# Both states of a head made by one product, with e^s stationary and k and v side by side

## The chip, the cores and the metric

The kernel runs on one core of a Trainium2 chip. The metric is the device time of one execution in microseconds (us).

## The reference

Input x is (4, 512, 512): 4 sequences of 512 tokens. There are 16 heads, with 128 columns of k and v each and 64 slots. All is float32.

```python
q = rope(x @ Wq.T); k = rope(x @ Wk.T); v = x @ Wv.T; g = x @ Wg.T     # per head (t, 128)
s = clip(x @ Ws1.T @ Ws2.T + bs2, -32, 32)                             # per head (t, 64)
es = exp(s); enz = exp(-cumlogsumexp(s, over t))
A  = tril(q @ k.T) * 128**-0.5
ok = enz * (A @ es)
qv = softmax(ok, over the 64 slots)
W2 = tril((qv * enz) @ es.T)
o  = W2 @ v
o  = o * rsqrt(mean(o * o) + 1e-5) * g_norm_weight * silu(g)
x  = layernorm(x + o @ Wo.T)
x  = layernorm(x + x @ (weight * scale_weight[:, None]).T + bias)
```

## The kernel before

Time is cut into chunks of 128 tokens (P = 128): 4 chunks to a sequence, 16 in all. The heads are cut into 4 groups of 4 heads (HG = 4). One step works on one chunk for one group: 64 steps, numbered i = 1 to 64. Within a sequence c = 0 to 3 is the number of the chunk. Causal sums over earlier chunks are not formed from scratch: after each chunk with c < 3 two states of each head are brought up to date, s1 = sum of k^T e^s (128 x 64) and s2 = sum of (e^s)^T v (64 x 128). A step with c > 0 adds the product of q with s1 to ok, and the product of qv * enz with s2 to o.

Each engine has its program in straight order, and semaphores join them; an engine does nothing out of its order. TensorE's order in `step`: `project_q` of the step after the next (24 matmuls of 256 columns, L958 to L961), ok of the own chunk (L1092), ok from s1 (L1096, c > 0), transposes of o_gated of the step before (L973), in the steps up to i = 14 `low_rank` (L1008), then the projection of k of the next step (L941, 12 matmuls of 512 columns), transposes of ok (L1119), slots, projection of v, transposes of prob, the output projection of the step before, W2 (L1159), o from s2 (L1163), sums of e^s (L986), projection of g, transposes of k_rot, o of the own chunk (L1183), the states (L1188 and L1193, c < 3), and the scores of the next step (L999).

PSUM is eight banks. `bank_c` holds the two accumulators of the states; ACT copies it to `states` in SBUF (L500, 128x512). `bank_e` holds the sums of e^s and their transposes.

The rest of a step that matters here: after L1183 ACT squares o (L662), DVE makes o_gated (L905), sums the squares (L907) and makes var (L910), POOL raises it to the power -1/2 (L461) and multiplies o_gated by it (L463); then o_gated can be transposed (L973) in the next step. DVE masks the scores (`mask_a`, L762) after var, before L1092 can run. In a step with c = 0 DVE then makes the low half of the output weights (L916, 128x2048).

Projections are made in the rounded type float32r, with every factor split into a high and a low half and three products; the matmuls around the states are float32. A matmul with 64 stationary columns writes to 64 of the 128 partitions, and the heads h even and h odd write to different halves.

The states before the change:

```python
for h in range(HG):
    pe.matmul(s1_acc[:, M * h:M * h + M], k_rot[now][:, P * h:P * h + P], es[now][:, M * h:M * h + M], ...)
for h in range(HG):
    mm = pe.matmul(s2_acc[rows, at], es[now][:, M * h:M * h + M], v[now][:, DV * h:DV * h + DV], ...)
```

In `pe.matmul(out, a, b)` a is the stationary operand and b the moving one.

Of the kernel before, what the change touches and what calls it, by code (L numbers as in the profile page):

```python
# [21 lines left out]
P = 128  # L22
# [3 lines left out]
HG = 4  # L26
# [28 lines left out]
def gated_slot_attention_block(nc, hs_cols, hs_rows, w_groups, ws1, small_in, ffn_w, ffn_scale, ffn_bias, out):  # L55
    with ExitStack() as ctx:
# [6 lines left out]
        def sem(name):  # L63
# [25 lines left out]
        masked, o_sq, kT = [sb(n, F)[:, :] for n in ("masked", "o_sq", "kT")]  # L89
        v, gate = [[sb(f"{n}{s}", F)[:, :] for s in range(2)] for n in ("v", "gate")]  # L90
        prob, okT, s_clip = [sb(n, H)[:, :] for n in ("prob", "okT", "s_clip")]
# [6 lines left out]
        rope_a, rope_b = sb("rope_a", F), sb("rope_b", F)  # L98
        k_rot = [sb(f"k_rot{s}", F) for s in range(2)]
        es_hi = [sb(f"es_hi{s}", H, F32R) for s in range(2)]  # L100
# [7 lines left out]

        pT, states = sb("pT", H), sb("states", 2 * H)
        s1, s2 = states[:, 0:H], states[:, H:2 * H]  # L110
        o_gated = sb("o_gated", F)
# [7 lines left out]
            bank(n) for n in ("bank_qv", "bank_kg", "bank_t", "bank_a", "bank_c", "bank_e")]  # L119
        s1_acc, s2_acc = bank_c[:, 0:H], bank_c[:, H:2 * H]  # L120

# [34 lines left out]
        def quarters(t):  # L156
# [3 lines left out]
        x1_bias, y_row, z = [[t[:, :] for t in four] for four in (  # L160
            (qT[0][:, 0:D], k_rot[0], k_rot[1], qT[0][:, D:2 * D]), (kT, v[0], v[1], o_sq), (gate[0], gate[1], masked, rope_a))]
        banks_T, banks_ffn = (bank_c, bank_e, bank_a, bank_s), (bank_qv, bank_kg, bank_t, bank_o)
# [3 lines left out]
        for name in ("first", "second"):  # L166
# [19 lines left out]
            sem(n) for n in ("a_mm", "okT_mm", "w2_mm", "o_mm", "states_mm", "sumT_mm")]  # L186
        kT_mm, pT_mm, ok_mm, oT_mm = [sem(n) for n in ("kT_mm", "pT_mm", "ok_mm", "oT_mm")]
        q_turned, q_summed, k_turned, k_summed = [sem(n) for n in ("q_turned", "q_summed", "k_turned", "k_summed")]
# [105 lines left out]
        def staged(t, s, lag):  # L294

            return t - lag, (s - lag) % LAST, not isinstance(t, int) or 0 <= t - lag < CHUNKS

        block = ctx.enter_context(nc.Block())
# [114 lines left out]
        def _(pool):  # L413
# [13 lines left out]
            def k_sum(slot, n):  # L427
                pool.wait_ge(k_turned, n)
                pool.tensor_tensor(k_rot[slot][:, :], rope_a[:, :], rope_b[:, :], ALU.add).then_inc(k_summed, 1)  # L429

# [67 lines left out]
        def _(act):  # L498
# [76 lines left out]
            hs_split(4)  # L575
            from_bank(v[0][:, :], bank_qv[:, :], v_mm, 1, v_made)
            act.wait_ge(g_mm, 1)
# [34 lines left out]
            def step(u, g, b, c, last, left):  # L612
# [3 lines left out]
                if c % 2 and i + 4 <= STEPS:  # L616
                    hs_split(i + 3)
                if not left:
                    tick(1, 1)
# [18 lines left out]
                if left:  # L638
                    exp_s((c + 1) % 2, n)
                    from_bank(v[(c + 1) % 2][:, :], bank_qv[:, :], v_mm, n, v_made)  # L640
                if last and c == 2:
# [295 lines left out]
        def _(pe):  # L937
# [32 lines left out]

            def transposes(src, n=HG):
                for h in range(n):
                    mm = pe.transpose(bank_t[:, P * h:P * h + P], src[:, P * h:P * h + P], ident)  # L973
                return mm
# [5 lines left out]
            def turn_and_sum(slot, n):  # L980

                pe.wait_ge(es_hi_made, n)
                pe.wait_ge(es_lo_made, n)
                for r in range(2):
                    for x, half in enumerate((es_hi, es_lo)):
                        mm = pe.matmul(bank_e[:, 2 * P * r:2 * P * r + 2 * P], half[slot][:, P * r:P * r + P],  # L986
                                       ident_keep[:, :], start=x == 0, stop=x == 1)
                mm.then_inc(sumT_mm, 1)

            def qT_of(j, h):  # L990
# [51 lines left out]
            pe.wait_ge(k_summed, 1)  # L1042
            transposes(k_rot[0]).then_inc(kT_mm, 1)
            pe.wait_ge(q_turned, 2)
# [23 lines left out]
            def step(u, g, b, c, last, left):  # L1068
# [14 lines left out]
                if not left:  # L1083
                    pe.wait_ge(states_made, carried(u, c - 1))
                    turn_x1(0, 0)
                pe.wait_ge(a_masked, i)
                if c:
                    pe.wait_ge(states_made, carried(u, c - 1))

                for h in range(HG):  # L1090
                    head = slice(P * h, P * h + P)
                    mm = pe.matmul(okT_of(h), es[now][:, M * h:M * h + M], masked[:, head], start=h < 2,  # L1092
                                   stop=c == 0, skip_group_check=True)
                if c:
                    for h in range(HG):
                        mm = pe.matmul(okT_of(h), s1[:, M * h:M * h + M], qT_of(i, h), start=False, stop=True,  # L1096
                                       skip_group_check=True)
                mm.then_inc(okT_mm, 1)

                if i > 1:  # L1100
                    pe.wait_ge(o_norm_made, i - 1)
                    transposes(o_gated).then_inc(oT_mm, 1)
                if i + 2 <= CHUNKS:
                    low_rank(now)
# [55 lines left out]
                if c:  # L1160
                    for h in range(HG):
                        rows, at = slice(64 * (h % 2), 64 * (h % 2) + 64), slice(P * (h // 2), P * (h // 2) + P)
                        mm = pe.matmul(o_of(h), pT[rows, at], s2[rows, at], start=False, stop=False,  # L1163
                                       skip_group_check=True)
                mm.then_inc(w2_mm, 1)
                if left:
                    pe.wait_ge(cumsT_made, 2 * i)
                    turn_and_sum(nxt, n)

                    pe.wait_ge(k_turned, n)  # L1170
                    if last and c == CB - 1:
                        w_ready(g * 4 + 4, g * 3 + 3)
                    project(WG, bank_kg, n).then_inc(g_mm, 1)
                    pe.wait_ge(k_summed, n)
                    transposes(k_rot[nxt]).then_inc(kT_mm, 1)
                if not left:
# [4 lines left out]
                for h in range(HG):  # L1181
                    head = slice(P * h, P * h + P)
                    mm = pe.matmul(o_of(h), masked[:, head], v[now][:, head], start=False, stop=True,  # L1183
                                   skip_group_check=True)
                mm.then_inc(o_mm, 1)
                if c < CB - 1:
                    for h in range(HG):
                        pe.matmul(s1_acc[:, M * h:M * h + M], k_rot[now][:, P * h:P * h + P],  # L1188
                                  es[now][:, M * h:M * h + M], start=c == 0 and h == 0, stop=True,
                                  skip_group_check=True)  # L1190
                    for h in range(HG):
                        rows, at = slice(64 * (h % 2), 64 * (h % 2) + 64), slice(DV * (h // 2), DV * (h // 2) + DV)
                        mm = pe.matmul(s2_acc[rows, at], es[now][:, M * h:M * h + M], v[now][:, DV * h:DV * h + DV],  # L1193
                                       start=False, stop=True, skip_group_check=True)
                    mm.then_inc(states_mm, 1)
# [103 lines left out]
```

## Time and profile before

| What | Value |
|---|---|
| median of 3 runs | 1460.3 us (1459.96 to 1460.4) |
| the profiled execution | 1457.91 us |
| its span, first to last instruction | 1456.1 us |
| TensorE matmuls busy | 1426.3 us (98%), 9664 records |
| DVE, POOL, ACT busy | 951.5, 521.1, 491.3 us |
| mean granted TensorE clock | 0.996 of full speed |

A float32 matmul leaves two records in the trace, one of the rounded type or a transpose one. A record of TensorE begins when its matmul starts; its end is modelled, and records overlap. So the cost of a group is read as the distance from its first start to the first start of the next group.

### The profile page before, as it was taken

The page shows a single profiled execution, that of the slowest core. Times are in us where ns is not written, and L with a number is a line of the kernel's source. Part 1 is how long each engine was busy: PE and PEld are TensorE (multiplying, and loading weights), DVE is VectorE, ACT ScalarE, POOL GpSimd, SP SyncE. Part 2 cuts the span into 40 slices and gives each one's busy share as a digit, 9 for nine tenths or more (in the row PEclk, how much of TensorE's full clock was granted, in tenths as well). Part 3 has the DMA queues.
Part 4 walks back from the last instruction along what each step waited for, and adds up shares of the span by engine and source line. Part 5 has one row for each costly group of instructions (what it writes and reads, how often), then busy time and mean ns, then how long its engine had stood idle before and what let it go on. Part 6 is the DMA issues. An engine that isn't in the chain of part 4 may idle for free.

```text
span 1456.1 us, 23764 instructions
## 1 busy us (share of the span) xinstructions
PE 1426.3 (98%) x9664; PEld 1204.2 (83%) x9664; DVE 951.5 (65%) x1635; ACT 491.3 (34%) x965; POOL 521.1 (36%) x440
## 2 busy tenths in 40 slices
PE   5999999999999999999999999999999999999988
PEld 4888888888888888888888888888888888888876
DVE  5756666566765666567765656657675666657677
ACT  4323223233322323223432322223432222323356
POOL 3322333334433333234533323334432333333255
PEclk9999999999999999999999999999999999999999
DMA  5210111113211201112211110222222021201223
GB/s 203 81 36 33 66 44 59 37 64 120 75 69 44 72 23 55 62 57 97 102 66 30 54 64 26 70 73 67 87 80 66 24 72 44 69 26 66 66 99 118
DMA packets 39562, 97.06 MB, mean 67 GB/s; under 512 B 4384, under 2 KB 4512, under 8 KB 35616
## 3 DMA queue, kind: packets, MB, share of 16 engines
q1 hardware_dynamic: 36864, 90.85, 18.7%
q10 hardware_dynamic: 2592, 4.72, 0.9%
q8 instruction: 76, 1.25, 0.4%
q14 instruction: 30, 0.25, 0.1%
HBM read 74.58 MB, written 20.97 MB: 66 GB/s over the span
## 4 chain that ended last, share of the span: by engine, by line
PE 85%; POOL 7%; DVE 3%; issue 2%; ACT 2%; DMA 0%; POOLq 0%; SPq 0%; ACTq 0%; DVEq 0%
PE bank_kg L941 25%; PE bank_qv L941 13%; PE bank_a L941 12%; PE bank_t L973 6%; POOL o_gated L463 5%; PE bank_wo L1183 4%; PE bank_e L986 3%; PE bank_wo L1159 3%; POOL rms L461 2%; PE bank_a L999 2%; PE bank_qv L958 2%; PE bank_qv L960 2%; PE bank_qv L961 2%; PE bank_c L1188 2%; DVE sum_sq L907 2%
## 5 line engine op out<-in xcount | busy, mean ns | idle before, releaser
L461 POOL TENSOR_TENSOR rms<-var,minus_half 128x4 f32<-128x4 f32 x64 | 65.1, 1017 | 537.3 <-DVE var L910 537.3
L941 PE MATMUL bank_kg<-w_hi,hs_hi 128*128 128x512 f32 x512 | 207.9, 406 | 2.0 <-DVE w_lo L677 1.9
L941 PE MATMUL bank_kg<-w_hi,hs_lo 128*128 128x512 f32 x512 | 202.7, 396 | 0.0
L941 PE MATMUL bank_kg<-w_lo,hs_hi 128*128 128x512 f32 x512 | 201.9, 394 | 0.0
L941 PE MATMUL bank_a<-wo_hi,oT 128*128 128x512 f32 x512 | 174.6, 402 | 0.0
L958 PE MATMUL bank_qv<-hs_hi,w_hi 128*128 128x256 f32 x504 | 146.5, 291 | 9.0 <-DVE w_lo L677 9.0
L758 DVE RECIPROCAL enzT<-cumsT 128x256 f32<-128x256 f32 x64 | 112.2, 1752 | 63.8 <-ACT cumsT L551 51.7
L429 POOL TENSOR_TENSOR k_rot<-rope_a,rope_b 128x512 f32<-128x512 f32 x64 | 82.7, 1292 | 183.4 <-DVE rope_b L706 183.4
L960 PE MATMUL bank_qv<-hs_lo,w_hi 128*128 128x256 f32 x504 | 141.1, 280 | 0.0
L961 PE MATMUL bank_qv<-hs_hi,w_lo 128*128 128x256 f32 x504 | 141.0, 280 | 0.0
L424 POOL TENSOR_TENSOR qT<-rope_a,rope_b 128x512 f32<-128x512 f32 x64 | 82.7, 1292 | 160.7 <-DVE rope_b L718 160.7
L500 ACT ACTIVATE oT<-bank_t 128x512 fp32r<-128x512 f32 x63 | 37.6, 598 | 279.9 <-PE bank_t L973 279.9
L941 PEld LDWEIGHTS bank_kg<-w_hi,hs_lo 128*128 128x128 f32 x512 | 96.1, 188 | 23.1
L941 PEld LDWEIGHTS bank_kg<-w_hi,hs_hi 128*128 128x128 f32 x512 | 96.2, 188 | 22.4 <-issue 3.9
L941 PEld LDWEIGHTS bank_a<-wo_hi,oT 128*128 128x128 f32 x512 | 96.2, 188 | 18.6
L941 PEld LDWEIGHTS bank_kg<-w_lo,hs_hi 128*128 128x128 f32 x512 | 96.3, 188 | 17.6
L941 PE MATMUL bank_qv<-w_hi,hs_hi 128*128 128x512 f32 x256 | 102.7, 401 | 2.8 <-DVE w_lo L677 2.6
L895 DVE TENSOR_TENSOR part<-bank_a,part 128x512 f32<-128x512 f32 x63 | 43.4, 689 | 91.7 <-PE bank_a L941 91.7
L958 PEld LDWEIGHTS bank_qv<-hs_hi,w_hi 128*128 128x128 f32 x504 | 95.2, 189 | 9.0 <-issue 9.0
L941 PE MATMUL bank_qv<-w_lo,hs_hi 128*128 128x512 f32 x256 | 102.2, 399 | 0.0
L941 PE MATMUL bank_qv<-w_hi,hs_lo 128*128 128x512 f32 x256 | 102.1, 399 | 0.0
L418 POOL TENSOR_TENSOR hs_lo<-hs_raw,hs_hi 128x512 fp32r<-128x512 f32 x64 | 97.4, 1523 | 12.3 <-ACT hs_hi L500 12.3
(172 smaller groups left out, 3225.3 us busy)
## 6 DMA issues: line engine op xcount, KB each, us to landing
w_raw<-w_groups SPq DMA_DIRECT2D x28, 1024.0 KB, 5.0
hs_raw<-hs_cols SPq DMA_DIRECT2D x64, 256.0 KB, 2.8
x_scratch<-part SPq DMA_DIRECT2D x64, 256.0 KB, 2.0
part<-x_scratch SPq DMA_DIRECT2D x48, 256.0 KB, 2.8
part<-hs_rows SPq DMA_DIRECT2D x16, 256.0 KB, 3.0
w_raw<-x_scratch SPq DMA_DIRECT2D x16, 256.0 KB, 3.1
w_raw<-w_groups SPq DMA_DIRECT2D x14, 256.0 KB, 6.1
out<-gate ACTq DMA_DIRECT2D x8, 256.0 KB, 2.1
```

The source lines that it names most:

```text
L418: pool.tensor_tensor(in_pair(hs_lo, j), tiles_of(hs_raw[(j - 1) % 2][:, :]), in_pair(hs_hi, j).bitcast(F32), ALU.subtract).then_inc(hs_lo_ ...
L424: pool.tensor_tensor(qT[pair % 2][:, F * half:F * half + F], rope_a[:, :], rope_b[:, :], ALU.add).then_inc(q_summed, 1)
L429: pool.tensor_tensor(k_rot[slot][:, :], rope_a[:, :], rope_b[:, :], ALU.add).then_inc(k_summed, 1)
L461: pool.tensor_tensor(rms[:, :], var[:, :], minus_half[:, :], ALU.pow).then_inc(rms_made, 1)
L463: pool.tensor_tensor(per_head(o_gated[:, :]), per_head(o_gated[:, :]), over_columns(rms[:, :], DV), ALU.mult).then_inc(o_norm_made, 1)
L758: dve.reciprocal(enzT[:, :], cumsT[slot][:, :])
L941: mm = pe.matmul(dst, x, y, start=start and n == 0, stop=stop and n == 2, **kw)
L958: pe.matmul(out_cols, w_hi[WQ][:, w_cols], hi, start=k == 0 and x == 0, stop=False, skip_group_check=True)
L960: pe.matmul(out_cols, w_hi[WQ][:, w_cols], lo, start=False, stop=False, skip_group_check=True)
L961: mm = pe.matmul(out_cols, w_lo[WQ][:, w_cols], hi, start=False, stop=k == KT - 1, skip_group_check=True)
L973: mm = pe.transpose(bank_t[:, P * h:P * h + P], src[:, P * h:P * h + P], ident)
L1183: mm = pe.matmul(o_of(h), masked[:, head], v[now][:, head], start=False, stop=True, skip_group_check=True)
```

## The change

The product with k stationary goes. One product per head has e^s stationary (128 x 64) and k and v side by side moving (128 x 256), and gives both states with the 64 slots on the partitions: (e^s)^T k and (e^s)^T v. For that k (after rotation) and v lie in one buffer `kv`, head by head. s1 is needed with the 128 columns of k on the partitions, so in the next step TensorE turns the k half back with two transposes of 128 x 128 (two heads each) into `bank_e`, and ACT copies the result (128x256) to `s1`. The product of s1 with q (L1096 before) moves behind the transposes of o_gated and waits for that copy.

```diff
-        k_rot = [sb(f"k_rot{s}", F) for s in range(2)]
+        kv = [sb(f"kv{s}", 2 * F)[:, :] for s in range(2)]
-        pT, states = sb("pT", H), sb("states", 2 * H)
-        s1, s2 = states[:, 0:H], states[:, H:2 * H]
+        pT, states, s1 = sb("pT", H), sb("states", 2 * H), sb("s1", H)
-        s1_acc, s2_acc = bank_c[:, 0:H], bank_c[:, H:2 * H]
+        s1_acc = bank_e[:, 0:H]
+        def kv_of(slot, which):
+            return kv[slot].rearrange("p (h e x) -> p h e x", e=2, x=P)[:, :, which, :]
...
-                pool.tensor_tensor(k_rot[slot][:, :], rope_a[:, :], rope_b[:, :], ALU.add).then_inc(k_summed, 1)
+                pool.tensor_tensor(kv_of(slot, 0), per_head(rope_a[:, :]), per_head(rope_b[:, :]), ALU.add).then_inc(k_summed, 1)
...
+                if c:
+                    from_bank(s1[:, :], s1_acc, s1_mm, carried(u, c - 1), s1_made)
                 if not left:
                     tick(1, 1)
...
-                    from_bank(v[(c + 1) % 2][:, :], bank_qv[:, :], v_mm, n, v_made)
+                    from_bank(kv_of((c + 1) % 2, 1), per_head(bank_qv[:, :]), v_mm, n, v_made)
...
-                pe.wait_ge(a_masked, i)
                 if c:
                     pe.wait_ge(states_made, carried(u, c - 1))
+                    pe.wait_ge(cumsT_made, 2 * i)
+                    for r in range(2):
+                        mm = pe.transpose(s1_acc[:, P * r:P * r + P], states[:, 2 * P * r:2 * P * r + P], ident)
+                    mm.then_inc(s1_mm, 1)
+                pe.wait_ge(a_masked, i)
 
                 for h in range(HG):
                     head = slice(P * h, P * h + P)
                     mm = pe.matmul(okT_of(h), es[now][:, M * h:M * h + M], masked[:, head], start=h < 2,
                                    stop=c == 0, skip_group_check=True)
+                if not c:
+                    mm.then_inc(okT_mm, 1)
+
+                if i > 1:
+                    pe.wait_ge(o_norm_made, i - 1)
+                    transposes(o_gated).then_inc(oT_mm, 1)
                 if c:
+                    pe.wait_ge(s1_made, carried(u, c - 1))
                     for h in range(HG):
                         mm = pe.matmul(okT_of(h), s1[:, M * h:M * h + M], qT_of(i, h), start=False, stop=True,
                                        skip_group_check=True)
-                mm.then_inc(okT_mm, 1)
-
-                if i > 1:
-                    pe.wait_ge(o_norm_made, i - 1)
-                    transposes(o_gated).then_inc(oT_mm, 1)
+                    mm.then_inc(okT_mm, 1)
...
-                        mm = pe.matmul(o_of(h), pT[rows, at], s2[rows, at], start=False, stop=False,
+                        mm = pe.matmul(o_of(h), pT[rows, at], s2_of(h), start=False, stop=False,
...
                 if c < CB - 1:
                     for h in range(HG):
-                        pe.matmul(s1_acc[:, M * h:M * h + M], k_rot[now][:, P * h:P * h + P],
-                                  es[now][:, M * h:M * h + M], start=c == 0 and h == 0, stop=True,
-                                  skip_group_check=True)
-                    for h in range(HG):
-                        rows, at = slice(64 * (h % 2), 64 * (h % 2) + 64), slice(DV * (h // 2), DV * (h // 2) + DV)
-                        mm = pe.matmul(s2_acc[rows, at], es[now][:, M * h:M * h + M], v[now][:, DV * h:DV * h + DV],
-                                       start=False, stop=True, skip_group_check=True)
+                        mm = pe.matmul(bank_c[64 * (h % 2):64 * (h % 2) + 64, 2 * P * (h // 2):2 * P * (h // 2) + 2 * P],
+                                       es[now][:, M * h:M * h + M], kv[now][:, 2 * P * h:2 * P * h + 2 * P],
+                                       start=c == 0 and h < 2, stop=True, skip_group_check=True)
                     mm.then_inc(states_mm, 1)
```

`s2_of(h)` is the v half of a head in the new layout of `states`. The buffers of the last phase that shared `k_rot` and `v` share `kv`.

## Rows read from the trace of the kernel before

**Rows 1.** The page, busy us (share of the span) and instructions.

```profile
PE 1426.3 (98%) x9664; PEld 1204.2 (83%) x9664; DVE 951.5 (65%) x1635; ACT 491.3 (34%) x965; POOL 521.1 (36%) x440
```

**Rows 2.** Timeline, POOL and DVE, c = 3: start, duration (us), engine, line.

```profile
705.61 1.04 POOL L463 TENSOR_TENSOR o_gated<-o_gated,rms 128x512 f32<-128x512 f32 x1
...
706.13 1.60 DVE L677 TENSOR_TENSOR w_lo<-w_raw,w_hi 128x1024 fp32r<-128x1024 f32 x1 [0.66 <-ACT w_hi L500]
```

**Rows 3.** Timeline, TensorE, start of the same step with c = 3.

```profile
707.17 0.28 PE L960 MATMUL bank_qv<-hs_lo,w_hi 128*128 128x256 f32 x1
707.29 0.28 PE L961 MATMUL bank_qv<-hs_hi,w_lo 128*128 128x256 f32 x1
707.50 0.66 PE L1092 MATMUL bank_wo<-masked,es 128*64 128x128 f32 x8
707.99 0.61 PE L1096 MATMUL bank_wo<-qT,states 128*64 128x128 f32 x8
708.52 0.66 PE L973 MATMUL bank_t<-small_ops,o_gated 128*128 128x128 f32 x4
708.94 0.48 PE L941 MATMUL bank_kg<-w_hi,hs_hi 128*128 128x512 f32 x1
```

**Rows 4.** Timeline, from c = 0 to c = 1: DVE, POOL, then TensorE.

```profile
745.73 0.16 DVE L910 SCALAR_TENSOR_TENSOR var<-sum_sq,eps_sum 128x4 f32<-128x4 f32 x1
746.30 0.69 DVE L762 TENSOR_TENSOR masked<-bank_a,small_ops 128x512 f32<-128x512 f32 x1 [0.41 <-PE bank_a L999]
746.91 2.34 DVE L916 SCALAR_TENSOR_TENSOR wo_lo<-w_raw,small_ops,wo_hi 128x2048 fp32r<-128x2048 f32 x1
...
746.04 1.02 POOL L461 TENSOR_TENSOR rms<-var,minus_half 128x4 f32<-128x4 f32 x1 [9.37 <-DVE var L910]
747.13 3.02 POOL L463 TENSOR_TENSOR o_gated<-o_gated,rms 128x512 f32<-128x512 f32 x1
...
749.51 0.61 PE L1096 MATMUL bank_wo<-qT,states 128*64 128x128 f32 x8
750.21 0.66 PE L973 MATMUL bank_t<-small_ops,o_gated 128*128 128x128 f32 x4
```

**Rows 5.** Timeline, TensorE, end of a step with c = 2.

```profile
702.06 1.00 PE L1188 MATMUL bank_c<-es,k_rot 128*128 128x64 f32 x8
702.99 0.66 PE L1193 MATMUL bank_c<-v,es 128*64 128x128 f32 x8
...
703.58 0.38 PE L999 MATMUL bank_a<-qT,kT 128*128 128x128 f32 x1
```

**Rows 6.** Timeline, four narrow windows, TensorE: the first start is the next record's.

```profile
318.68 0.33 PE L1193 MATMUL bank_c<-v,es 128*64 128x128 f32 x2
...
318.84 0.50 PE L1193 MATMUL bank_c<-v,es 128*64 128x128 f32 x6
...
318.95 0.39 PE L1193 MATMUL bank_c<-v,es 128*64 128x128 f32 x4
319.27 0.38 PE L999 MATMUL bank_a<-qT,kT 128*128 128x128 f32 x1
```

**Rows 7.** Line L1188: duration ns, minimum/median/maximum.

```profile
L1188 PE MATMUL bank_c<-es,k_rot x384: 222/275/276, 53.7 to 1381.1; 128*128 128x64 f32 x192
```

**Rows 8.** Timeline, TensorE: transposes of k_rot.

```profile
722.77 0.60 PE L973 MATMUL bank_t<-small_ops,k_rot 128*128 128x128 f32 x4
723.21 1.06 PE L1183 MATMUL bank_wo<-v,masked 128*128 128x128 f32 x8
```

**Rows 9.** Timeline, TensorE, a step with low_rank.

```profile
170.91 0.66 PE L973 MATMUL bank_t<-small_ops,o_gated 128*128 128x128 f32 x4
171.49 0.66 PE L1008 MATMUL bank_wo<-hs_raw,ws_raw 128*64 128x128 f32 x8
172.08 0.50 PE L941 MATMUL bank_kg<-w_hi,hs_hi 128*128 128x512 f32 x1
```

**Rows 10.** Timeline, TensorE, step 63 (idle before, and its releaser).

```profile
1365.05 0.66 PE L973 MATMUL bank_t<-small_ops,o_gated 128*128 128x128 f32 x4 [0.37 <-POOL o_gated L463]
```

**Rows 11.** Groups by form, ACT: busy us, mean ns, idle before, releaser.

```profile
L500 ACT ACTIVATE esT<-bank_e 128x256 f32<-128x256 f32 x64 | 24.1, 377 | 154.7 <-PE bank_e L986 154.7
```

More of the change, by code:

```diff
@@ L89, in gated_slot_attention_block @@
         masked, o_sq, kT = [sb(n, F)[:, :] for n in ("masked", "o_sq", "kT")]
-        v, gate = [[sb(f"{n}{s}", F)[:, :] for s in range(2)] for n in ("v", "gate")]
+        gate = [sb(f"gate{s}", F)[:, :] for s in range(2)]
+        kv = [sb(f"kv{s}", 2 * F)[:, :] for s in range(2)]
         prob, okT, s_clip = [sb(n, H)[:, :] for n in ("prob", "okT", "s_clip")]
@@ L160, in gated_slot_attention_block @@
         x1_bias, y_row, z = [[t[:, :] for t in four] for four in (
-            (qT[0][:, 0:D], k_rot[0], k_rot[1], qT[0][:, D:2 * D]), (kT, v[0], v[1], o_sq), (gate[0], gate[1], masked, rope_a))]
+            (qT[0][:, 0:D], kv[0][:, 0:D], kv[1][:, 0:D], qT[0][:, D:2 * D]), (kT, kv[0][:, D:2 * D], kv[1][:, D:2 * D], o_sq), (gate[0], gate[1], masked, rope_a))]
         banks_T, banks_ffn = (bank_c, bank_e, bank_a, bank_s), (bank_qv, bank_kg, bank_t, bank_o)
@@ L186, in gated_slot_attention_block @@
             sem(n) for n in ("a_mm", "okT_mm", "w2_mm", "o_mm", "states_mm", "sumT_mm")]
-        kT_mm, pT_mm, ok_mm, oT_mm = [sem(n) for n in ("kT_mm", "pT_mm", "ok_mm", "oT_mm")]
+        kT_mm, pT_mm, ok_mm, oT_mm, s1_mm = [sem(n) for n in ("kT_mm", "pT_mm", "ok_mm", "oT_mm", "s1_mm")]
+        s1_made = sem("s1_made")
         q_turned, q_summed, k_turned, k_summed = [sem(n) for n in ("q_turned", "q_summed", "k_turned", "k_summed")]
@@ L575, in _ @@
             hs_split(4)
-            from_bank(v[0][:, :], bank_qv[:, :], v_mm, 1, v_made)
+            from_bank(kv_of(0, 1), per_head(bank_qv[:, :]), v_mm, 1, v_made)
             act.wait_ge(g_mm, 1)
@@ L969, in project, with transposes @@
                 return mm
-            def transposes(src, n=HG):
+            def transposes(src, n=HG, apart=P):
                 for h in range(n):
-                    mm = pe.transpose(bank_t[:, P * h:P * h + P], src[:, P * h:P * h + P], ident)
+                    mm = pe.transpose(bank_t[:, P * h:P * h + P], src[:, apart * h:apart * h + P], ident)
                 return mm
@@ L988, in turn_and_sum, with s2_of @@
                 mm.then_inc(sumT_mm, 1)
+            def s2_of(h):
+                at = 2 * P * (h // 2) + P
+                return states[64 * (h % 2):64 * (h % 2) + 64, at:at + P]
             def qT_of(j, h):
@@ L1042, in _ @@
             pe.wait_ge(k_summed, 1)
-            transposes(k_rot[0]).then_inc(kT_mm, 1)
+            transposes(kv[0], apart=2 * P).then_inc(kT_mm, 1)
             pe.wait_ge(q_turned, 2)
@@ L1174, in step @@
                     pe.wait_ge(k_summed, n)
-                    transposes(k_rot[nxt]).then_inc(kT_mm, 1)
+                    transposes(kv[nxt], apart=2 * P).then_inc(kT_mm, 1)
                 if not left:
@@ L1182, in step @@
                     head = slice(P * h, P * h + P)
-                    mm = pe.matmul(o_of(h), masked[:, head], v[now][:, head], start=False, stop=True,
+                    mm = pe.matmul(o_of(h), masked[:, head], kv[now][:, 2 * P * h + P:2 * P * h + 2 * P], start=False, stop=True,
                                    skip_group_check=True)
```

## The prediction

> **What bounds the kernel now.** I read the page first, then the waits by engine, then the timeline of the stretches that the change touches. The page says that TensorE is busy for 1426.3 us, 98% of the span [rows 1]: nothing on another engine matters unless it makes TensorE wait. In the view of waits almost nothing did; what the reader must look for is the start of each group of matmuls against the end of what it needs. Two such places turn up, both at the transposes of o_gated (L973), which need POOL's product L463. In the steps with c = 2 and 3 that product is ready long before: it ends at 706.65 (705.61 + 1.04) [rows 2] and L973 starts at 708.52 [rows 3], 1.87 us later. In the steps with c = 1 it ends at 747.13 + 3.02 = 750.15, and L973 starts at 750.21 [rows 4]: TensorE waits there. The gap from L1096 to L973 is 0.70 us (749.51 to 750.21) where it is 0.53 with c = 3 [rows 3, 4], so 0.16 of wait in each of the 16 steps with c = 1. The product takes 3.02 us there, and not 1.04, because DVE's L916 (2.34 us, from 746.91) runs beside it: it ends 0.90 us after L916 does (749.25) [rows 4].
>
> **Prices of TensorE.** A float32 matmul is two records. Of a stationary operand 128 wide they follow each other by 0.11 us: 8 of L1188 take 0.93 us [rows 5]. With 64 wide ones on the two halves of the columns, records start in pairs: at 318.68 (x2), 318.84 (x6 are left), 318.95 (x4 are left), one more pair, and L999 at 319.27 [rows 6]. L1092 gives the last pair's place: its four slots before L1096 are 0.49 [rows 3], 0.16 + 3 x 0.11. So a pair slot is 0.11 us for 128 moving columns, the first is 0.05 longer, and of the 0.59 to L999 there remain 0.21 from the last pair to the next full-width matmul, 0.10 more than a slot. Going in costs 0.09 (L961 to L1092 is 0.21; from L960 to L961, 256 columns of the rounded type, 0.12) [rows 3]. A switch into the 64-wide form and out again thus costs some 0.3 us.
>
> **The end of a step (c = 0, 1, 2: 48 of 64).** Removed: 4 matmuls with k stationary (8 records, 0.93) and 4 with e^s stationary over v (0.59), together 1.52 us from 702.06 to 703.58 [rows 5]. Added: 4 matmuls with e^s stationary over 256 columns of k and v, float32: 8 records, 4 pair slots. No row has a float32 moving operand of 256 columns, so the slot is bounded. Below: 0.11, if the present slot were set by the two loads. Above: 0.44, if the pairs did not run together at this width. For the value I take the moving columns at two cycles each: the first record of L1188, with 64 columns, lasts 222 ns, the usual one 275 [rows 7], where the later ones wait for their loads: 53 ns for 64 columns, so 256 columns cost 0.107 more than 128, a slot of 0.22. Then: going in 0.09, first slot 0.27, two of 0.22, last slot and way out 0.32: 1.12 us. Saved: 0.40 us. The product that was limited by its 128-wide load (0.11 for 64 columns) now rides in the paired form.
>
> **The start of the next step (c = 1, 2, 3).** Added are two transposes of states before L1092: four of k_rot take 0.44 [rows 8], so 0.11 each, and the way from them into the 64-wide form 0.20 (as from L973 into L1008: 0.58 less three transposes of 0.11 and 0.05 for the first) [rows 9]. From the last L961 to L1092 it is then 0.12 + 0.11 + 0.20 = 0.43 instead of 0.21. Moved: L1096 goes behind the transposes of o_gated. L1092 to L973: 0.16 + 2 x 0.11 + 0.21 = 0.59; L973 to L1096: 0.58 [rows 9]; L1096 to L941: 0.59, as L1008 to L941 [rows 9]. Sum 2.19 us from L961 to the first L941, where before it is 708.94 - 707.29 = 1.65 [rows 3]: +0.54. While low_rank (L1008) still stands there (up to i = 14), the move makes no new switch, since L1096 joins its form: L1096 to L1008 is 0.49, and the sum is +0.27.
>
> So with c = 2 and 3: six steps with low_rank at 0.27 - 0.40 = -0.13 are -0.8 us; 24 without at 0.54 - 0.40 = +0.14 are +3.4. POOL's product keeps more than a microsecond of its 1.87.
>
> **The same with c = 1.** L973 starts when L463 lets it, so what TensorE saves before it is lost unless L463 comes earlier, while what is moved behind it (L1096) is paid in full: 0.58 + 0.59 in place of the 0.42 from L973 to L941, +0.75; with low_rank +0.49. Does L463 come earlier? mask_a (L762) starts 0.41 after DVE is free, held by the scores, which come 0.40 earlier; it can start at 745.89, when L910 is done [rows 4]. L916 follows 0.61 later, at 746.51 instead of 746.91. If it then runs its 2.34 us, L463 and L973 come 0.40 earlier. But POOL's L461 runs from 746.04 to 747.06 [rows 4], and with the change it is under way when L916 starts. The nearest row: the w_lo half at 706.13 starts 0.52 before POOL's L463 ends and ends 1.08 after it (1.60 us) [rows 2]; a half of 1024 columns was held for POOL's operation. Held like this, L916 would end 747.06 + 2 x 1.08 = 749.22, not 749.25: 0.03 gained. Bounds: 0.03 and 0.40. I take 0.03, though L461 is a tiny operation (128x4) and may not hold DVE. So 12 steps at +0.72 are +8.6, four with low_rank at +0.46 are +1.8.
>
> The Trainium skill (SBUF — State Buffer, section "SBUF: two separate sides") says that whichever of a DVE operation with two SBUF inputs and a GpSimd operation starts first holds the shared port for its whole instruction. By that the sum is as I have it; no row here shows L461 holding anything.
>
> **The last two steps** (i = 63, 64) have no project_q, and L973 waits for L463 in both (0.37 us of idle at 1365.05) [rows 10]. The two new transposes hide in the wait for a_masked; the moved L1096 does not: +0.75, and +0.9 in the last, where okT (0.42 on DVE) is also late for L1119. Together +1.7.
>
> **What is hidden.** s1_made: the second transpose ends 0.50 after the last L961 starts (0.12 + 0.11 + a record's 0.27), ACT's copy of 128x256 takes 0.38 [rows 11], so with the hand-overs it is there at 1.0; L1096 comes at 1.60. ACT sits idle at that place. Without cover each tenth costs 48 x 0.1 = 4.8 us. Later okT_mm: DVE is busy with rotate_q until about then, and TensorE has the 12 records of project(WK) before it needs ok_scaled. k_sum and the copy of v write the same number of columns in strips of 128; they are not waited for. cumsT_made is a step old. The copy of states is as large as before. No DMA changes.
>
> **Sum:** -0.8 + 3.4 + 8.6 + 1.8 + 1.7 = +14.7 us. The profiled execution took 1457.9 us for its span of 1456.1; it becomes 1472.6. The median of the runs shown is 2.4 above it: 1475 us.
>
> **Rivals.**
> *L461 does not hold L916.* For it: it is 128x4 and may touch SBUF for a moment only. Against: the row of 1.60 us. Then c = 1 costs 0.75 - 0.40 = +0.35 twelve times and +0.09 four times, 4.6 in place of 10.4: 1469 us. Chance 0.3.
> *The slot stays at 0.11 (not slower).* If two parallel loads and not the moving columns set the 0.11, the states cost 0.44 less: for the 30 steps with c = 2 and 3 that are not last, -13.2 us; 1462 us, or 1456 if L461 does not hold either. It decides from a slot of 0.12 down. Against it: the 53 ns above. Chance 0.09 in both forms.
> *The pairs fall apart at 256 columns:* eight records of 0.22, 0.87 more than forecast for each of 48. Steps with c = 2 and 3 then pay 6 x 0.74 + 24 x 1.01; with c = 1 L916 starts 0.47 later, behind POOL's L463, whose wait of 0.16 is gone, so that they pay 12 x 0.85 + 4 x 0.58. With the last two that is +43: 1503 us. Against: L1193 pairs in its four slots, and L1008 has the same 0.59. Chance 0.03.
> *s1_made is late:* if ACT's copy came 0.4 after TensorE wants it, 48 x 0.4 = 19 us: 1494. Against: 0.6 us of slack. Chance 0.04.
>
> The Trainium skill (TensorEngine Tiling (Array Packing), section "Performance Considerations") recommends exactly this swap for a right-hand side of 64 columns or fewer, at up to twice the speed. By it the k half would fall from 0.93 to 0.47, some 22 us over 48 steps, which is what my 0.40 holds less its switches; it counts neither transposes nor moved matmuls.
>
> **How the numbers follow.** My forecast has 0.5, and 0.04 is left for what I do not see. The predicted time is 1475. With the slot at 0.23 (9% over the pure count, as the rounded type shows with 0.12 for 256 columns) the sum is 3 us higher; with L461 not holding and small gains it reaches 1467. The range is 1466 to 1480. I count 0.2% (2.9 us) as no change: of the cases only the 0.11 slot ends there or below, 0.05 within and 0.04 faster; with what is not seen, 0.05, 0.06 and 0.89.
>
> **What the profile after would show.** L999 comes 1.23 us after the last L1183 record where it was 1.63. The e^s records start in pairs 0.22 apart. L973 (o_gated) to L941 is 1.17 instead of 0.42 from group 2 on. With c = 1, L916 lasts about 2.7 us if it is held by L461, and 2.34 if not; L1092 to L973 grows to some 1.3 us if it is. POOL's L463 stays at 1.04 with c = 2, 3. ACT's s1 copy ends before the last transpose of o_gated. I am wrong if slots are not 0.22, or if L1096 waits.

## The result and the profile after

The changed kernel takes 1465.59 us (median of 6 runs, 1464.88 to 1467.1) against 1460.13 us before: a ratio of 1.0041, with a 95% interval of 1.003 to 1.0052. It is slower, as forecast, but by 5.5 us and not by 14.7, and lies 0.4 us below the range. Every ratio in this document leaves out one execution of a later kernel that took 1750.49 us at a mean granted clock of 0.753.

The page after; busy us (share of the span) and instructions:

```profile
span 1465.3 us, 23236 instructions
...
PE 1431.4 (98%) x9376; PEld 1175.5 (80%) x9376; DVE 943.2 (64%) x1635; ACT 509.6 (35%) x1013; POOL 515.0 (35%) x440
```

TensorE is the bound as it was [rows 1]. The end of a step, to be read against [rows 5]: the timeline of TensorE, with start and duration in us; the rows with x4 and x2 come from narrow windows, which show where the pairs start.

```profile
704.15 0.28 PE L1200 MATMUL bank_wo<-kv,masked 128*128 128x128 f32 x1
704.36 1.08 PE L1207 MATMUL bank_c<-kv,es 128*64 128x256 f32 x8
...
704.62 0.60 PE L1207 MATMUL bank_c<-kv,es 128*64 128x256 f32 x4
...
705.05 0.39 PE L1207 MATMUL bank_c<-kv,es 128*64 128x256 f32 x2
705.37 0.38 PE L1009 MATMUL bank_a<-qT,kT 128*128 128x128 f32 x1
```

Eight records still start in pairs: the first at 704.36, then 704.62, the last at 705.05. So slots are 0.26, 0.22 and 0.22 (0.43 for the two), and 0.32 to the next full-width matmul; from the last L1200 to L1009 it is 1.22 us, where 1.23 was forecast. This part of the sum was right to 0.01 us a step.

The start of a step with c = 3, against [rows 3], in the same view:

```profile
709.08 0.28 PE L967 MATMUL bank_qv<-hs_hi,w_lo 128*128 128x256 f32 x1
709.20 0.38 PE L1100 MATMUL bank_e<-small_ops,states 128*128 128x128 f32 x2
709.51 0.66 PE L1106 MATMUL bank_wo<-masked,es 128*64 128x128 f32 x8
710.10 0.66 PE L979 MATMUL bank_t<-small_ops,o_gated 128*128 128x128 f32 x4
710.68 0.66 PE L1117 MATMUL bank_wo<-qT,s 128*64 128x128 f32 x8
711.27 0.50 PE L947 MATMUL bank_kg<-w_hi,hs_hi 128*128 128x512 f32 x1
```

2.19 us from L967 to L947, as forecast, where it was 1.65. ACT's copy (L504) is there in time:

```profile
709.62 0.38 ACT L504 ACTIVATE s<-bank_e 128x256 f32<-128x256 f32 x1 [1.21 <-PE bank_e L1100]
```

It ends at 710.00, 0.68 before L1117 starts.

The way from c = 0 to c = 1, against [rows 4]: DVE, then POOL, then TensorE.

```profile
747.88 0.16 DVE L916 SCALAR_TENSOR_TENSOR var<-sum_sq,eps_sum 128x4 f32<-128x4 f32 x1
748.04 0.69 DVE L768 TENSOR_TENSOR masked<-bank_a,small_ops 128x512 f32<-128x512 f32 x1
748.64 2.34 DVE L922 SCALAR_TENSOR_TENSOR wo_lo<-w_raw,small_ops,wo_hi 128x2048 fp32r<-128x2048 f32 x1
...
748.19 1.02 POOL L465 TENSOR_TENSOR rms<-var,minus_half 128x4 f32<-128x4 f32 x1 [9.38 <-DVE var L916]
749.28 2.60 POOL L467 TENSOR_TENSOR o_gated<-o_gated,rms 128x512 f32<-128x512 f32 x1
...
750.98 0.66 PE L1106 MATMUL bank_wo<-masked,es 128*64 128x128 f32 x8
751.94 0.66 PE L979 MATMUL bank_t<-small_ops,o_gated 128*128 128x128 f32 x4 [0.30 <-POOL o_gated L467]
752.52 0.66 PE L1117 MATMUL bank_wo<-qT,s 128*64 128x128 f32 x8
753.11 0.50 PE L947 MATMUL bank_kg<-w_hi,hs_hi 128*128 128x512 f32 x1
```

Here the forecast failed. The mask (L768) is no longer held by the scores and L922 (L916 before) follows at 748.64, 0.45 after POOL's L465 (L461 before) began, while in [rows 4] it began 0.87 after it. It still takes 2.34 us, as before the change. So L465 held nothing from there on: L1106 to L979 is 0.96 us, where some 1.3 was forecast for a hold. L467 is then blocked for a shorter time (2.60 us where it was 3.02), TensorE gets it 0.42 us earlier, and the saving of step c = 0 survives. All 16 began 0.45 to 0.46 us into L465, and their durations (line L922, ns: minimum/median/maximum) leave no room for a hold in any of them:

```profile
L922 DVE SCALAR_TENSOR_TENSOR wo_lo<-w_raw,small_ops,wo_hi x16: 2341/2342/2344, 57.6 to 1347.4; 128x2048 fp32r<-128x2048 f32 x16
```

The Trainium skill (SBUF — State Buffer, section "SBUF: two separate sides") says that the first of the two holds the port for its whole instruction. The row of 1.60 us [rows 2] fits that, and so does the same place in the changed kernel, where the DVE operation starts earlier against POOL's product and takes 2.01 us:

```profile
707.92 2.01 DVE L683 TENSOR_TENSOR w_lo<-w_raw,w_hi 128x1024 fp32r<-128x1024 f32 x1 [0.66 <-ACT w_hi L504]
707.81 1.04 POOL L467 TENSOR_TENSOR o_gated<-o_gated,rms 128x512 f32<-128x512 f32 x1
```

Both DVE operations end 1.08 us after POOL's product does. The pair of L465, 4 elements a partition, and L922 does not fit the rule.

### The profile page after: what moved, and what is told of

Its sections match the earlier page's. It is cut to its first block, busy times and chain, and to the rows that moved or that the text cites. A ratio compares the mean times of both kernels' runs of the same rounds, so it can differ in the third digit from the quotient of the medians.

```text
span 1465.3 us, 23236 instructions
## 1 busy us (share of the span) xinstructions
PE 1431.4 (98%) x9376; PEld 1175.5 (80%) x9376; DVE 943.2 (64%) x1635; ACT 509.6 (35%) x1013; POOL 515.0 (35%) x440
## 4 chain that ended last, share of the span: by engine, by line
PE 87%; POOL 6%; DVE 3%; issue 2%; ACT 1%; DMA 0%; POOLq 0%; SPq 0%; ACTq 0%; DVEq 0%
PE bank_kg L947 25%; PE bank_qv L947 13%; PE bank_a L947 12%; PE bank_t L979 6%; PE bank_wo L1200 4%; POOL o_gated L467 4%; PE bank_e L992 3%; PE bank_wo L1176 3%; PE bank_a L1009 3%; PE bank_qv L964 2%; PE bank_qv L966 2%; PE bank_qv L967 2%; PE bank_c L1207 2%; POOL rms L465 2%; PE bank_wo L1117 2%
## 5 line engine op out<-in xcount | busy, mean ns | idle before, releaser
L465 POOL TENSOR_TENSOR rms<-var,minus_half 128x4 f32<-128x4 f32 x64 | 65.1, 1018 | 536.7 <-DVE var L916 536.7
L947 PE MATMUL bank_kg<-w_hi,hs_hi 128*128 128x512 f32 x512 | 209.1, 408 | 2.0 <-DVE w_lo L683 1.9
L947 PE MATMUL bank_kg<-w_hi,hs_lo 128*128 128x512 f32 x512 | 203.0, 397 | 0.0
L947 PE MATMUL bank_kg<-w_lo,hs_hi 128*128 128x512 f32 x512 | 202.3, 395 | 0.0
L947 PE MATMUL bank_a<-wo_hi,oT 128*128 128x512 f32 x512 | 174.3, 401 | 0.0
L433 POOL TENSOR_TENSOR kv<-rope_a,rope_b 128x512 f32<-128x512 f32 x64 | 82.7, 1293 | 210.2 <-DVE rope_b L712 210.2
L964 PE MATMUL bank_qv<-hs_hi,w_hi 128*128 128x256 f32 x504 | 146.7, 291 | 9.2 <-DVE w_lo L683 9.2
L966 PE MATMUL bank_qv<-hs_lo,w_hi 128*128 128x256 f32 x504 | 141.4, 281 | 0.0
L967 PE MATMUL bank_qv<-hs_hi,w_lo 128*128 128x256 f32 x504 | 141.4, 280 | 0.0
L947 PEld LDWEIGHTS bank_kg<-w_hi,hs_hi 128*128 128x128 f32 x512 | 96.4, 188 | 29.1 <-issue 10.6
L947 PEld LDWEIGHTS bank_kg<-w_hi,hs_lo 128*128 128x128 f32 x512 | 96.3, 188 | 22.9
L947 PEld LDWEIGHTS bank_a<-wo_hi,oT 128*128 128x128 f32 x512 | 96.2, 188 | 18.4
L947 PEld LDWEIGHTS bank_kg<-w_lo,hs_hi 128*128 128x128 f32 x512 | 96.6, 189 | 17.5
L643 ACT ACTIVATE prob<-prob 128x256 f32<-128x256 f32 x64 | 26.8, 418 | 230.3 <-DVE prob L871 230.3
L947 PE MATMUL bank_qv<-w_hi,hs_hi 128*128 128x512 f32 x256 | 102.3, 400 | 2.6 <-DVE w_lo L683 2.6
L964 PEld LDWEIGHTS bank_qv<-hs_hi,w_hi 128*128 128x128 f32 x504 | 95.4, 189 | 9.2 <-issue 9.2
L947 PE MATMUL bank_qv<-w_lo,hs_hi 128*128 128x512 f32 x256 | 101.9, 398 | 0.0
L947 PE MATMUL bank_qv<-w_hi,hs_lo 128*128 128x512 f32 x256 | 101.9, 398 | 0.0
```

The costliest lines, as they stand in the source:

```text
L433: pool.tensor_tensor(kv_of(slot, 0), per_head(rope_a[:, :]), per_head(rope_b[:, :]), ALU.add).then_inc(k_summed, 1)
L465: pool.tensor_tensor(rms[:, :], var[:, :], minus_half[:, :], ALU.pow).then_inc(rms_made, 1)
L947: mm = pe.matmul(dst, x, y, start=start and n == 0, stop=stop and n == 2, **kw)
L964: pe.matmul(out_cols, w_hi[WQ][:, w_cols], hi, start=k == 0 and x == 0, stop=False, skip_group_check=True)
L966: pe.matmul(out_cols, w_hi[WQ][:, w_cols], lo, start=False, stop=False, skip_group_check=True)
L967: mm = pe.matmul(out_cols, w_lo[WQ][:, w_cols], hi, start=False, stop=k == KT - 1, skip_group_check=True)
```

## The experiments

Each kernel was timed beside the kernel before (median 1459.43 us for the first four, 1458.95 for the rest); ratios are to that.

**Only the product moved.** The kernel before, with this edit alone:

```diff
+                if not c:
+                    mm.then_inc(okT_mm, 1)
+                if i > 1:
+                    pe.wait_ge(o_norm_made, i - 1)
+                    transposes(o_gated).then_inc(oT_mm, 1)
                 if c:
                     for h in range(HG):
                         mm = pe.matmul(okT_of(h), s1[:, M * h:M * h + M], qT_of(i, h), ...)
-                mm.then_inc(okT_mm, 1)
-                if i > 1:
-                    pe.wait_ge(o_norm_made, i - 1)
-                    transposes(o_gated).then_inc(oT_mm, 1)
+                    mm.then_inc(okT_mm, 1)
```

> The kernel before, in which only the product of s1 with q (L1096) is moved behind the transposes of o_gated; states as before, no turning back. Theory (the move is what costs): two more switches between the 64-wide and the full form, +0.33 us in each of 24 steps with c = 2 and 3 outside the low_rank steps, +0.05 in 6 with low_rank, +0.75 (12) and +0.49 (4) with c = 1, where the product lies behind a transpose that waits for POOL anyway, +1.7 to 3.2 in the last two steps: +21 to +22.5 us, 1481 to 1483 us. Rival (the move is free, since TensorE only trades places, and the cost of the change is the turning back): within 3 us of before. In the profile the theory wants L973 to the first L941 at 1.17 us.

Measured: 1478.55 us, ratio 1.013 (1.0115 to 1.0146), +19.1 us. Compared step by step with the trace of before (from scores to scores), steps with c = 2 and 3 cost 0.35 more, with low_rank nothing, c = 1 0.78 and 0.42, and step 63 2.3. The three steps with c = 3 at a change of group cost only 0.06. That is under the 21 to 22.5 us expected: the three steps at a change of group are 0.8 cheaper than expected, and the last two cost 1.1 and not 1.7 to 3.2, once the 1.5 us of a halved clock in step 63 of this profile are taken off (see below). The move is by far the dearest part of the change; the rival is out.

**Only the states.** The changed kernel without the transposes into `bank_e` and without ACT's copy, in the old order:

```diff
-                    pe.wait_ge(cumsT_made, 2 * i)
-                    for r in range(2):
-                        mm = pe.transpose(s1_acc[:, P * r:P * r + P], states[:, 2 * P * r:2 * P * r + P], ident)
-                    mm.then_inc(s1_mm, 1)
...
-                        mm = pe.matmul(okT_of(h), s1[:, M * h:M * h + M], qT_of(i, h), ...)
+                        mm = pe.matmul(okT_of(h), states[:, M * h:M * h + M], qT_of(i, h), ...)
```

> The changed kernel's states (e^s stationary over k and v side by side), but the order of before, no turning back and no copy: the product with q takes the k half as it lies, so that this part of the output is not the reference's. Theory (0.41 us saved at the end of each of 48 steps, and in c = 1 DVE's L916 starts that much earlier, so that the saving survives there too): -19.7 us, 1440.5 us. Rival (my prediction: POOL's L461 holds DVE, and the saving of 16 steps is lost in the wait for L463): -13 us, 1447 us. A second rival (the slot is not what it seems once the other costs are away): any other time.

Measured: 1440.94 us, ratio 0.9875 (0.986 to 0.989), -18.5 us. Every step with c = 0, 1 and 2 is 0.41 us shorter (0.39 to 0.44), but for step 63, whose start waits for POOL; the steps with c = 3 are as before, except that three of them, at a change of group, are 0.4 longer. That c = 1 keeps its saving is what separates this from my prediction's 1447. In the three steps at a change of group the saving meets a real hold. TensorE waits 0.43 us there, before the projection of v, for DVE's `w_lo` (L681). Its first half now starts 0.41 earlier against POOL's product, is held until that ends, and takes 2.01 us where it took 1.60 [rows 2]. So in these steps the time is set by `w_lo`, and what TensorE does at their start costs less.

**The states turned early.** The changed kernel with the transposes in the middle of `project_q` and the product back in its place:

```diff
                     for k in range(KT):
                         mm = project_q(i + 2, bank_qv, k)
+                        if k == KT - 1:
+                            mm.then_inc(q_mm, 1)
+                        if k == 1 and c:
+                            turn_s1(u, c, i)
-                    mm.then_inc(q_mm, 1)
...
-                if not c:
-                    mm.then_inc(okT_mm, 1)
-
-                if i > 1:
-                    pe.wait_ge(o_norm_made, i - 1)
-                    transposes(o_gated).then_inc(oT_mm, 1)
                 if c:
                     pe.wait_ge(s1_made, carried(u, c - 1))
                     for h in range(HG):
                         mm = pe.matmul(okT_of(h), s1[:, M * h:M * h + M], qT_of(i, h), ...)
-                    mm.then_inc(okT_mm, 1)
+                mm.then_inc(okT_mm, 1)
+
+                if i > 1:
+                    pe.wait_ge(o_norm_made, i - 1)
+                    transposes(o_gated).then_inc(oT_mm, 1)
```

`turn_s1` holds the waits and the two transposes; in the last two steps it stands before L1112 (the own chunk's product).

> The changed kernel with the two transposes put into the middle of project_q, after its second quarter, and the product of s1 back in its old place right behind L1092. Theory: the turning back costs its 0.22 us and nothing else, the copy on ACT is done long before the product, no new switch: 30 steps with c = 2 and 3 at 0.22 - 0.41 = -0.19, 16 with c = 1 at -0.34 (the old wait of 0.155 for POOL is used up as well), the last two steps at about nothing: -11 us, 1449 us. Rival (the turning back itself is dear, because ACT's copy or the hand-over of bank_e holds TensorE): no faster than before. If the clock drop of step 63 comes from the long wait there, the granted clock stays at 1.0 in this kernel.

Measured: 1447.67 us, ratio 0.9922 (0.9908 to 0.9935), -11.8 us: faster than both kernels. The timeline of TensorE around the transposes and at the start of the same step with c = 3:

```profile
701.81 0.28 PE L967 MATMUL bank_qv<-hs_hi,w_lo 128*128 128x256 f32 x1
701.93 0.38 PE L1082 MATMUL bank_e<-small_ops,states 128*128 128x128 f32 x2
702.07 0.36 PE L964 MATMUL bank_qv<-hs_hi,w_hi 128*128 128x256 f32 x1
702.27 0.28 PE L966 MATMUL bank_qv<-hs_lo,w_hi 128*128 128x256 f32 x1
...
703.45 0.28 PE L967 MATMUL bank_qv<-hs_hi,w_lo 128*128 128x256 f32 x1
703.65 0.66 PE L1112 MATMUL bank_wo<-masked,es 128*64 128x128 f32 x8
704.14 0.61 PE L1117 MATMUL bank_wo<-qT,s 128*64 128x128 f32 x8
704.68 0.66 PE L979 MATMUL bank_t<-small_ops,o_gated 128*128 128x128 f32 x4
705.09 0.48 PE L947 MATMUL bank_kg<-w_hi,hs_hi 128*128 128x512 f32 x1
```

From L967 to L947 it is 1.64 us, as before the change [rows 3], and the transposes cost 0.22: from L1082 over L964 to L966 it is 0.34, where L964 alone takes 0.12. Steps with c = 2 are 0.19 shorter, with c = 1 0.35, both as expected.

**The old order, the transposes where the change has them:** the same second hunk as above, without the first.

> The changed kernel with the transposes where they are, but the product of s1 right behind L1092 as before, so that it must wait for ACT's copy. Theory: the copy is done about 0.98 us after the last record of project_q starts (0.50 until the second transpose ends, 0.38 the copy, 0.1 for the hand-overs), the product could start at 0.92: some 0.1 us of wait, dearer than nothing but cheaper than the two switches of the move: c = 2 and 3 at -0.09, c = 1 at -0.24: -6.6 us, 1453.5 us. Rival (the wait for the copy is long, so that the move was worth its price): slower than the changed kernel, over 1466 us, which takes a wait of over 0.5 us.

Measured: 1452.52 us, ratio 0.9955 (0.9939 to 0.997), -6.9 us, as expected. L1106 to the product is 0.55 us (705.01 to 705.56) instead of 0.49: the wait that the move avoids is 0.06 us. A start with c = 3 costs 0.34 us here and 0.22 with the states turned early, so the wait and what follows from it are 0.12; in the changed kernel it costs 0.54.

```profile
705.01 0.66 PE L1106 MATMUL bank_wo<-masked,es 128*64 128x128 f32 x8
705.56 0.66 PE L1111 MATMUL bank_wo<-qT,s 128*64 128x128 f32 x8
```

**The changed kernel again.**

> The changed kernel once more, for a second profile and a tighter interval. Theory (its steps are as in the first profile, the rest of the difference between profile and median lies in the first 37 us and in step 63, where the granted clock fell): a median 5 to 7 us above before; every step with c = 1, 2, 3 as in the first profile to 0.03 us; the clock falls in step 63 again, since the wait there is the same. Rival (the steps themselves vary by microseconds): other steps differ.

Measured: 1465.31 us, ratio 1.0044 (1.003 to 1.0058), span 1463.2. The steps repeat the first profile to 0.04 us, except step 63: there it is 0.78 us longer than before, in the first profile 2.30. In both TensorE waits 1.22 us for L467, after a wait of 0.56 and of 0.57 for the mask. TensorE in step 63 of the first profile, and then of this one:

```profile
1371.66 0.96 PE L979 MATMUL bank_t<-small_ops,o_gated 128*128 128x128 f32 x4 [1.22 <-POOL o_gated L467]
1372.56 1.12 PE L1117 MATMUL bank_wo<-qT,s 128*64 128x128 f32 x8
```

```profile
1371.12 0.66 PE L979 MATMUL bank_t<-small_ops,o_gated 128*128 128x128 f32 x4 [1.22 <-POOL o_gated L467]
1371.71 0.66 PE L1117 MATMUL bank_wo<-qT,s 128*64 128x128 f32 x8
```

The windows of the two (busy us and count of PE, PEld, DVE, ACT and POOL, the granted clock, DMA) show why; the first fence is the first profile:

```profile
1371.60:1373.60 2.00, 1.94 (x12) 1.28 (x12) 0.00 (x0) 0.60 (x1) 0.01 (x1) 0.57 0.00 0
1373.60:1375.60 2.00, 2.00 (x7) 1.65 (x6) 1.02 (x2) 0.00 (x0) 0.00 (x0) 0.58 0.00 0
```

```profile
1372.00:1374.00 2.00, 2.00 (x15) 1.55 (x12) 1.02 (x2) 0.42 (x1) 0.00 (x0) 1.00 0.00 0
1374.00:1376.00 2.00, 2.00 (x12) 1.61 (x11) 0.38 (x1) 0.00 (x0) 0.00 (x0) 1.00 0.00 0
```

In the first profile the granted clock was half (1.2 GHz) for 3.4 of these 4 us, which is what shares of 0.57 and 0.58 come to; in the other it was full (2.4 GHz), after the same waits. It cost 1.5 us once and nothing once. My expectation that it would fall again was wrong. Of the other kernels with the product moved, it fell in step 63 of two profiles and stayed in one; in the three kernels with the product in its old place and the states turned it stayed full in step 63, and the wait for the product of POOL is 0.79 there. But with the states turned early it fell at about 1378.9 in step 64, late in a wait for `w_lo`; with the old order, where the clock did not fall in step 64, the wait is the same. The view of the windows of the first, and TensorE at the end of the wait in the first and in the second:

```profile
1378.90:1380.90 2.00, 1.36 (x3) 1.16 (x4) 1.55 (x6) 0.47 (x2) 1.09 (x2) 0.52 0.00 0
```

```profile
1379.54 0.76 PE L947 MATMUL bank_qv<-w_hi 128*128 128x512 f32 x1 [2.18 <-DVE w_lo L683]
```

```profile
1383.30 0.47 PE L947 MATMUL bank_qv<-w_hi 128*128 128x512 f32 x1 [2.18 <-DVE w_lo L683]
```

So the clock did not stay at 1.0 in the kernel with the states turned early, as I had expected if the long wait in step 63 were the cause. It fell in step 64 too in the profiles of the states alone and of the kernel named "Both" below. Which wait brings it down is not shown.

**The output weights' low half later.** The changed kernel, with this edit in DVE's order:

```diff
                 if i > 1:
                     lo(oT_lo, bank_t[:, :], oT_hi, oT_hi_made, i - 1, oT_lo_made)
+                if c == 1:
+                    dve.wait_ge(wo_hi_made, u + 1)
+                    dve.scalar_tensor_tensor(wo_lo[:, :], w_raw[0][:, :], gn, ...).then_inc(wo_lo_made, 1)
...
                 if left:
                     mask_a(n)
-                if c == 0:
-                    dve.wait_ge(wo_hi_made, u + 1)
-                    dve.scalar_tensor_tensor(wo_lo[:, :], w_raw[0][:, :], gn, ...).then_inc(wo_lo_made, 1)
```

> The changed kernel with DVE's low half of the output weights (L922) moved from the end of the step with c = 0 to the step with c = 1, behind the low half of o_gated. Theory (with c = 1 TensorE waits 0.37 us for POOL's product, which L922 holds up): the product takes 1.04 us in all steps, the wait goes, -0.37 x 16 = -5.9 us against the changed kernel, so about level with before (1459 to 1461 us). Rival (L922 in its new place delays DVE's softmax work or POOL's sums, and TensorE waits for those): no faster than the changed kernel.

Measured: 1462.15 us, ratio 1.0023 (1.0013 to 1.0032), 3.2 us under the changed kernel and 1.2 above the range expected. POOL's product takes 1.04 us in all 64 steps:

```profile
L467 POOL TENSOR_TENSOR o_gated<-o_gated,rms x64: 1038/1040/1041, 57.8 to 1405.1; 128x512 f32<-128x512 f32 x64
```

Fourteen of the steps with c = 1 are 0.35 to 0.41 us shorter than in the changed kernel; steps 2 and 14 are 0.06 and 0.49 longer. By steps it is -4.9 us. L979 comes 0.37 us earlier in both of those steps too, but in step 2 the transposes of prob come 0.36 late, and in step 14 L992 waits 0.80 for POOL's es_lo (L437). So it is L922 that makes L979 late in c = 1, and the wait is 0.37; the new place has a price of its own.

**Both.** The kernel with the states turned early, and this edit as well.

> The kernel with the early turning back (the fastest so far, 11.8 us under before), with the low half of the output weights moved as well. Theory: there the start of step c = 1 is no longer bound by POOL's product but by TensorE's own order, so nothing is left to gain: within 1 us of the kernel with the early turning back, 1447 to 1449 us. Rival (POOL's product still binds): -0.1 to -0.4 us in 16 steps, up to 6 us faster.

Measured: 1452.96 us, ratio 0.9956 (0.9943 to 0.997), 5.3 us slower than without. Nine of the 16 steps with c = 1 are -0.35 as they were without it, so POOL's product binds no more there, as expected. But steps 2, 6, 10, 14, 30, 46 and 62, in the first group or ahead of a change of group or of the end, are 0.2 to 1.1 us longer than there: TensorE waits for what comes late behind the moved operation, prob in steps 2, 6, 10 and 14, es_lo in steps 14, 30, 46 and 62. The view of waits has two rows that the kernel without the edit does not have:

```profile
PE bank_e L992 <- POOL es_lo L437: 2.3, 4, 0.8
PEld bank_t L979 <- ACT prob L643: 2.1, 4, 0.8
```

In step 30 DVE's next `w_lo` and POOL's es_lo now start together, and es_lo takes 2.86 us where it takes 0.75 in step 22 of the same kernel:

```profile
670.05 2.28 DVE L683 TENSOR_TENSOR w_lo<-w_raw,w_hi 128x2048 fp32r<-128x2048 f32 x1
670.06 2.86 POOL L437 TENSOR_TENSOR es_lo<-es,es_hi 128x256 fp32r<-128x256 f32 x1
```

It is the same block as that of L467 by L922, in another place. By steps it is 3.7 us; the remaining 1.6 of the 5.3 lie outside the steps compared or between sessions and are not explained. The expectation was wrong in the sum: it asked only what the edit frees.

**Swapped, but not side by side.** e^s stationary, k and v in two products of 128 columns:

```diff
-                    for h in range(HG):
-                        mm = pe.matmul(bank_c[64 * (h % 2):64 * (h % 2) + 64, 2 * P * (h // 2):2 * P * (h // 2) + 2 * P],
-                                       es[now][:, M * h:M * h + M], kv[now][:, 2 * P * h:2 * P * h + 2 * P],
-                                       start=c == 0 and h < 2, stop=True, skip_group_check=True)
+                    for x in range(2):
+                        for h in range(HG):
+                            at = 2 * P * (h // 2) + P * x
+                            mm = pe.matmul(bank_c[64 * (h % 2):64 * (h % 2) + 64, at:at + P],
+                                           es[now][:, M * h:M * h + M], kv[now][:, 2 * P * h + P * x:2 * P * h + P * x + P],
+                                           start=c == 0 and h < 2 and x == 0, stop=True, skip_group_check=True)
```

> The changed kernel, with e^s stationary as there, but k and v not side by side: two products of 128 moving columns for each head instead of one of 256, so twice the loads. Theory (the pair slot goes by the moving columns, 0.11 us for 128): 0.16 + 6 x 0.11 + 0.21 = 1.03 us against 1.01, +0.5 us in all, not measurable; what saves the 0.41 is the swap, not the width. Rival (loads set the slot, and one load for 256 columns is what saves): the eight pairs take 0.9 us more per step, +43 us, or at least several us.

Measured: 1467.85 us, ratio 1.0059 (1.004 to 1.0077), 2.5 us over the changed kernel, with intervals that overlap. By steps each end of a step is 0.02 us longer than with one product, 1.0 us in all. So the swap saves 0.39 of the 0.41 us; joining k and v saves 0.02. Twice the loads cost next to nothing; with one load each, the slot is 0.11 for 128 moving columns here and 0.22 for 256 in the changed kernel, so it goes with the columns.

## Why the prediction was wrong

In its own terms, against before, from the repeated profile. The change's cost at the start of a step is the step's difference plus the 0.41 that its end saves; as in the prediction, each start is set against the saving just ahead of it.

| Term | Forecast | Measured |
|---|---|---|
| 6 steps, c = 2 and 3, low_rank | -0.8 | -1.3 (-0.21 each) |
| 24 others, c = 2 and 3 | +3.4 | +2.6 (21 at +0.13, 3 at about -0.03) |
| 12 steps, c = 1 | +8.6 | +4.4 (+0.37 each) |
| 4 steps, c = 1, low_rank | +1.8 | 0.0 |
| last two steps | +1.7 | +1.1 |
| sum | +14.7 | +6.8 |

The step that failed is the one on L916: "Held like this, L916 would end 747.06 + 2 x 1.08 = 749.22". It is 6.0 of the 7.9 us. The runs showed in its place that L916 (L922 after) is not held: 2.34 us in 16 of 16, and the saving of 0.41 survives. My own rival had it: with L461 holding nothing, the 16 steps were to cost 4.6, and they cost 4.4. Its total of 1469 would still have been 3.4 too high. I took the nearest row, but it was of a POOL operation on 512 elements a partition; L461 works on 4. In the trace of before L916 and L461 overlap in all 16, by some 0.15 us, which is too short to show either answer; I should have said so and given the two cases equal weight in the range.

The rest is small. The last two steps were charged without the saving ahead of them, 0.6 of the error; three starts at a change of group cost 0.38 and not 0.54, which with 0.41 saved for 0.40 makes 0.8; with low_rank the start costs 0.20 and not 0.27, 0.5. The last 1.3 us, from 6.8 by steps to 5.5 by medians, are between two profiled executions and the medians; timed again, the medians differ by 6.4.

Two readings of the prediction were weaker than their result. The 53 ns that gave the slot of 0.22 are the difference between two records of 64 columns [rows 7] and say nothing of columns; I was lucky there. The records do bear the price out elsewhere: 222 ns for the first with 64 columns, 275 as the median of L1183 with 128, 379 as that of L1207 with 256. And the listed prices of going in and out add up to 0.24, not to "some 0.3"; the distances between groups, which the sum used, make the move 0.32 to 0.33, and it measured 0.35.

What was right: the 0.40 (0.41) with a slot of 0.22, the 0.54 at the start, the copy's slack, and that POOL's product keeps its lead with c = 2 and 3. The move of the product alone (+19.1) and the states alone (-18.5) leave 4.9 us of the measured 5.5 for turning back; 0.2 in 30 steps, hidden with c = 1, is 6. So the gain of the new states is real, and it is spent on the place of one group of four matmuls, which was moved to avoid a wait of 0.06 us: with the old order the same kernel is 13 us faster. By steps 8.3 of these lie in c = 1, where the moved product stands behind L979 and its wait, and only 0.20 a step in the others outside low_rank.

The profiled execution of before is 1.0 to 2.4 us under the medians. Its steps were the ones compared. All nine other profiles are longer than it in what comes before the first scores, by up to 1.9 us, and in what comes after the last, from 1381.86 us on, by 0.3 to 2.1. Of the latter, the three in which the clock fell in step 64 have 1.7 to 2.1 and the six others 0.3 to 0.7; what varies at the start is open. That the median of the changed kernel lies under its first profile agrees with a clock that falls in some executions only; it was not shown for unprofiled ones.

## What to carry to other kernels

Before a group of narrow matmuls is moved to hide a wait, price the wait and the two switches of the array's form: here 0.06 us of wait (0.12 with what follows it) against some 0.33, and far more where the moved group lands behind another wait. A place inside the full-width matmuls ahead costs neither. Where two engines' overlap decides, look at the ordering in all cases: an earlier start can shorten a block or meet another one, and the nearest row must be near in the thing that matters, here the operation that would hold. Ask of every operation moved out of the way what stands behind it in the new place.

## What was not expected of the hardware

A POOL operation of 128x4 that runs 1.02 us did not delay a DVE operation with two SBUF inputs that began 0.45 us into it (2.34 us, 16 times), while one of 128x512 held a DVE operation until its end: it took 1.60 us with 0.52 of overlap [rows 2] and 2.01 with 0.93, 1.08 after POOL's end both times. The two POOL operations differ in size and in kind (a power, a product), and no start nearer than 0.45 us to that of the small one occurs; which of these decides is not shown. The Trainium skill (TensorEngine Tiling (Array Packing), section "Key Properties") says that a change of tiling mode drains TensorE and the trace agrees as far as the price goes: a change into the 64-wide form and out again is some 0.3 us each time, 0.35 a step in the first experiment; the drain itself it does not show. After the same wait of 1.22 us and one of 0.56 us before it, the granted clock fell to half in one execution and stayed full in another.
